# A language-model tower on one core: the filter network between the first groups, adjacency row blocks added on VectorE, seeds by square root

## The reference

```python
def _vgcn(word_emb, gv_ids, adj, W, b):
    ev = word_emb[gv_ids]
    H = jnp.einsum('bgh,bhd->bgd', adj, ev)
    g = H.mean(axis=1)
    return jax.nn.relu(g @ W.T + b)
# tok: x = concat(emb + pos, g1, g2, g3); y = layernorm(x @ W_proj.T + b_proj) * gamma + beta
def _implicit_filter(L, w1, b1, w2, b2, w3, b3, freq, deltas_abs):
    z, t = _pos_emb(L)
    h = jnp.sin(freq * (z @ w1.T + b1))
    h = jnp.sin(freq * (h @ w2.T + b2))
    h = h @ w3.T + b3
    decay = jnp.exp(-t[:, None] * deltas_abs[None, :])
    return h * (decay + SHIFT)
# attn: h = h + fft_conv(u, k) + u * bias, with u = layernorm(h)
# ffn:  top_k of xf @ Wr.T with k = 2, softmax over the two, gelu experts, weighted sum, h = h + out
```

## Time and profile before

| | |
|---|---|
| median of three runs | 1069.83 us (1067.11 to 1072.25) |
| profiled execution | 1066.09 us, of which the span of instructions is 1064.2 |
| group stage | the last projection ends at 376.8 us |
| conv, on TensorE | starts at 392.8 us |
| routing | about 443 to 514 us |
| first expert tile | 559 us |

### The profile page before, as it was taken

How to read it: one execution, slowest core, us unless ns; L and a number is a source line. 1 busy time by engine, 2 the same in 40 slices (tenths; PEclk the granted TensorE clock), 3 DMA queues, 4 the chain that set the end, 5 groups by cost and what they waited for, 6 DMA issues and landing times. The chain is left out here.

```text
span 1064.2 us, 22506 instructions
## 1 busy us (share of the span) xinstructions
PE 916.3 (86%) x7666; PEld 872.7 (82%) x7666; DVE 610.6 (57%) x1939; ACT 520.6 (49%) x1219; POOL 673.0 (63%) x592
## 2 busy tenths in 40 slices
PE   1999999999999939567259999999999999999993
PEld 0999999999999839567148899899889989999992
DVE  3046745666457664867864555556556655556561
ACT  2022222212223235698356666566656666666661
POOL 6767777677677000067015788778768768888864
PEclk9967655665557569879659999999999999999997
DMA  7427547266364339504944544764763463444442
GB/s 223 137 71 242 175 150 243 84 228 202 112 240 130 104 104 301 159 1 121 279 141 112 110 61 59 196 139 61 172 161 58 61 168 57 64 62 61 60 48 30
DMA packets 99495, 138.08 MB, mean 130 GB/s; under 512 B 13395, under 2 KB 81142, under 8 KB 97366
## 3 DMA queue, kind: packets, MB, share of 16 engines
q0 software_dynamic: 39552, 53.26, 26.1%
q1 hardware_dynamic: 58854, 73.40, 22.0%
q10 hardware_dynamic: 1008, 10.34, 2.7%
HBM read 98.14 MB, written 38.82 MB: 129 GB/s over the span
## 5 line engine op out<-in xcount | busy, mean ns | idle before, releaser
L893 ACT ACTIVATE Hs<-bank,U 128x256 bf16<-128x256 f32 x426 | 213.8, 502 | 176.6 <-PE bank L719 176.6
L518 POOL DMA_INDIRECT out<-Hs,id_s x142 | 235.7, 1660 | 64.9 <-issue 56.1
L1233 DVE TENSOR_TENSOR Hs<-Hs 128x512 bf16<-128x512 f32 x213 | 147.6, 693 | 174.9 <-ACT Hs L894 161.8
L484 POOL DMA_INDIRECT ev_g<-in_word_emb,ids_i x192 | 191.6, 998 | 71.4 <-issue 54.5
L894 ACT ACTIVATE Hs<-bank,U 128x256 f32<-128x256 f32 x426 | 216.2, 508 | 0.0
L509 POOL DMA_INDIRECT blob<-xtab_d,id_g x142 | 142.1, 1001 | 109.6 <-DVEq L1217 47.6
L734 PE MATMUL bank<-U,Hs 128*128 128x192 bf16 x852 | 210.0, 247 | 0.3 <-issue 0.3
L736 PE MATMUL bank<-U,Hs 128*128 128x192 bf16 x852 | 208.8, 245 | 0.0
L735 PE MATMUL bank<-U,Hs 128*128 128x192 bf16 x852 | 208.6, 245 | 0.0
L715 PE MATMUL bank<-blob,U 128*128 128x256 bf16 x426 | 117.1, 275 | 13.8 <-issue 11.8
L718 PE MATMUL bank<-blob,U 128*128 128x256 bf16 x426 | 117.1, 275 | 0.0
(11 more groups left out here) (192 smaller groups left out, 1699.9 us busy)
## 6 DMA issues: line engine op xcount, KB each, us to landing
adj_s<-in_adj SPq DMA_DIRECT2D x48, 256.0 KB, 7.6
ev_g<-kpad_d SPq DMA_DIRECT2D x24, 512.0 KB, 5.8
U<-blob_d SPq DMA_DIRECT2D x14, 771.0 KB, 4.9
wst<-in_wsrc SPq DMA_DIRECT2D x8, 1344.0 KB
blob_d<-blob ACTq DMA_DIRECT2D x7, 1443.0 KB, 5.6
U<-blob_d SPq DMA_DIRECT2D x14, 672.0 KB
xtab_d<-U SPq DMA_DIRECT2D x4, 1552.0 KB, 10.4
out<-Hs SPq DMA_DIRECT2D x4, 1536.0 KB, 10.9
```

The source lines that it names most:

```text
L484: pool.indirect_dma_start(ev_g[:, p, j, b, :], None, t["word_emb"], bass.IndirectOffsetOnAxis(ap=ids_i[:, 1 + j, i * Q + b:i * Q + b + 1], ...
L518: pool.indirect_dma_start(out, bass.IndirectOffsetOnAxis(ap=id_s[:, 2 * q + h:2 * q + h + 1], axis=0), yo[:, q % RX, h, :], None, compute_ ...
L893: f(hh[w][:, d, :], ps, ACT.Gelu, bias=bi[:, d:d + 1])
L1233: last = v.tensor_tensor(hl[w][:, c:c + 2, :], hf[w][:, c:c + 2, :], hh[w][:, c:c + 2, :], ALU.subtract)
```

## The change

The filter network's second and third layer move behind the first two groups: the second matmul behind the projection of group 0, the third before the projection of group 1, the sine and decay on ScalarE behind `graphs(0)`, VectorE's second argument and the taps behind `rows(0)`. Its sums move from bank 0 to bank 7 and its scratch from `ys` to the last eight batches of `Hs`. VectorE adds the four row blocks of each adjacency into the first (`row_sums`, two additions a group, the first of 128x768, the second of 128x384), and the column means read that block alone, one matmul a graph. ScalarE seeds the roots by a square root, VectorE takes its reciprocal. The share exponentials move from i = 6, 10, 14 to i = 9, 11, 14, and a dummy square root stands ahead of the first seeds.

```diff
@@ -538,28 +538,30 @@
             mm = nc.tensor.matmul
             pe.wait_ge(loaded, 16 * N_LOADS)
-            mm(bank[0][0:16, 0:128], w1T, net_z, start=True, stop=True).then_inc(filt_step, 1)
+            mm(bank[7][0:16, 0:128], w1T, net_z, start=True, stop=True).then_inc(filt_step, 1)
             nc.tensor.transpose(bank[1][:, 0:128], pos[:, 0:D0], cst[:, 0:128])
             nc.tensor.transpose(bank[1][0:D1, 128:256], pos[:, D0:D], cst[:, 0:128]).then_inc(pos_t, 1)
             pe.wait_ge(pos_ts, 1)
             mm(bank[2][:, 0:D], posT0[:, :], wp0[:, :], start=True, stop=False)
             mm(bank[2][:, 0:D], posT1[:, :], wp1[0:D1, :], start=False, stop=True).then_inc(pos_t, 1)
-            pe.wait_ge(filt_in, 1)
-            mm(bank[0][0:16, 128:256], w2T, sinb[:, 3, :], start=True, stop=True).then_inc(filt_step, 1)
-            pe.wait_ge(filt_in, 2)
-            mm(bank[0][:, 256:384], w3T[:, 0:D0], sinb[:, 4, :], start=True, stop=True)
-            mm(bank[0][0:D1, 384:512], w3T[:, D0:D], sinb[:, 4, :], start=True, stop=True).then_inc(filt_step, 1)
-            pe.wait_ge(kready, 2)
             pe.wait_ge(pos_done, 1)
             pe.wait_ge(cast_done, 1)
-            def column_means(n, i, p):
-                pe.wait_ge(adj_in[p], 16 * GRAPHS * n)
+            def filter_layer(n):
+                pe.wait_ge(filt_in, n)
+                if n == 1:
+                    mm(bank[7][0:16, 128:256], w2T, sinb[:, 3, :], start=True, stop=True).then_inc(filt_step, 1)
+                else:
+                    mm(bank[7][:, 256:384], w3T[:, 0:D0], sinb[:, 4, :], start=True, stop=True)
+                    mm(bank[7][0:D1, 384:512], w3T[:, D0:D], sinb[:, 4, :], start=True, stop=True).then_inc(filt_step, 1)
+                    pe.wait_ge(kready, 2)
+
+            def column_means(i, p):
+                pe.wait_ge(summed, i + 1)
                 after(pe, cs_ready, i)
                 for j in range(GRAPHS):
                     k = p * KG + j * Q
-                    for r in range(Q):
-                        last = mm(bank[0][:, k:k + Q], adj_s[:, p, j, r, :], mean_w[:, :], start=r == 0, stop=r == Q - 1)
+                    last = mm(bank[0][:, k:k + Q], adj_s[:, p, j, 0, :], mean_w[:, :], start=True, stop=True)
                 last.then_inc(colsum, 1)
             def turn_embeddings(it, i, p):
...
@@ -601,14 +603,19 @@
             def pair(it):
                 for p in range(2):
                     i = 2 * it + p
+                    opening = isinstance(it, int) and it == 0
                     turn_embeddings(it, i, p)
                     if not (isinstance(i, int) and i == NQ - 1):
-                        column_means(it + 1 + p, i + 1, 1 - p)
+                        column_means(i + 1, 1 - p)
                     graph_vectors(it, i, p)
                     graph_features(i)
+                    if opening and p == 1:
+                        filter_layer(2)
                     project(i, p)
-
-            column_means(1, 0, 0)
+                    if opening and p == 0:
+                        filter_layer(1)
+
+            column_means(0, 0)
             steps(pe, NQ // 2, pair, last=1)
...
@@ -752,15 +759,18 @@
             f(posT0[:, :], bank[1][:, 0:128], ACT.Copy)
             f(posT1[:, :], bank[1][0:D1, 128:256], ACT.Copy).then_inc(pos_ts, 1)
-            for n in range(2):
+            def filter_sine(n):
                 act.wait_ge(filt_arg, n + 1)
                 f(sinb[:, 3 + n, :], sinb[:, 2, :], ACT.Sin).then_inc(filt_in, 1)
+            def filter_decay():
+                trow = cst[:, 512:640]
+                f(dec[:, 0, :], trow, ACT.Exp, scale=filt[:, 0, 3:4])
+                f(dec[0:D1, 1, :], trow[0:D1, :], ACT.Exp, scale=filt[0:D1, 1, 3:4]).then_inc(dec_done, 1)
+
+            filter_sine(0)
             act.wait_ge(cast_done, 1)
             act.wait_ge(loaded, 16 * N_LOADS)
-            trow = cst[:, 512:640]
-            f(dec[:, 0, :], trow, ACT.Exp, scale=filt[:, 0, 3:4])
-            f(dec[0:D1, 1, :], trow[0:D1, :], ACT.Exp, scale=filt[0:D1, 1, 3:4]).then_inc(dec_done, 1)
             def column_copy(i, p):
                 act.wait_ge(colsum, i + 1)
...
@@ -802,6 +812,9 @@
                     if not (isinstance(i, int) and i == NQ - 1):
                         column_copy(i + 1, 1 - p)
                     graphs(i, p)
+                    if isinstance(i, int) and i == 0:
+                        filter_decay()
+                        filter_sine(1)
                     if p:
                         split_hi(it)
                     if not (isinstance(i, int) and i == 0):
...
@@ -832,9 +845,7 @@
                 first, n = PIECES[k]
                 b = slice(first, first + n)
                 act.wait_ge(var_ready, k + 1)
-                f(seed[:, 1, b], seed[:, 0, b], ACT.Ln, scale=-2.0).then_inc(log_done, 1)
-                act.wait_ge(log_done, k + 1)
-                f(seed[:, 2, b], seed[:, 1, b], ACT.Exp, scale=-0.5).then_inc(seed_ready, 1)
+                f(seed[:, 1, b], seed[:, 0, b], ACT.Sqrt, scale=-2.0).then_inc(seed_ready, 1)
             def row_parts(i):
                 p = i % 2
...
@@ -858,6 +869,7 @@
                 act.wait_ge(gap_ready, g + 1)
                 f(wsm[:, 1, bass.ds(g * GRP, GRP)], wsm[:, 0, bass.ds(g * GRP, GRP)], ACT.Exp).then_inc(exp_done, 1)
+            f(junk[:, :], mean_w[:, 0:1], ACT.Sqrt)
             seeds(0)
             seeds(1)
             row_parts(0)
...
@@ -868,8 +880,8 @@
                 turned_parts(i)
                 if i in (1, 4, 8):
                     seeds({1: 3, 4: 4, 8: 5}[i])
-                if i in (6, 10, 14):
-                    gap_exp((i - 6) // QG)
+                if i in (9, 11, 14):
+                    gap_exp((9, 11, 14).index(i))
             gap_exp(NG - 1)
             f(junk[:, :], mean_w[:, 0:1], ACT.Gelu)
...
@@ -930,10 +942,10 @@
             v.tensor_scalar(filt[0:D1, 1, 3:4], filt[0:D1, 1, 0:1], -1.0, None, ALU.mult).then_inc(cast_done, 1)
-            for n in range(2):
+            def filter_argument(n):
                 dve.wait_ge(filt_step, n + 1)
                 fence()
-                v.tensor_scalar(sinb[:, 0, :], bank[0][0:16, n * 128:(n + 1) * 128], net_cols[:, n:n + 1], net_cols[:, 2:3], ALU.add, ALU.mult)
+                v.tensor_scalar(sinb[:, 0, :], bank[7][0:16, n * 128:(n + 1) * 128], net_cols[:, n:n + 1], net_cols[:, 2:3], ALU.add, ALU.mult)
                 fence()
                 v.tensor_scalar(sinb[:, 1, :], sinb[:, 0, :], 1.0 / TWO_PI, MAGIC, ALU.mult, ALU.add)
                 fence()
...
@@ -947,16 +959,17 @@
                     src = sinb[:, 2, :]
                 fence()
                 v.tensor_scalar(sinb[:, 2, :], sinb[:, 2, :], 3.1415925, -3.1415925, ALU.min, ALU.max).then_inc(filt_arg, 1)
-            dve.wait_ge(filt_step, 3)
-            dve.wait_ge(dec_done, 1)
-
-            for c, n in ((0, D0), (1, D1)):
-                kk = kT[0:n, c, 0:S]
-                v.tensor_scalar(kk, bank[0][0:n, 256 + 128 * c:384 + 128 * c], filt[0:n, c, 1:2], 1.0 / NFFT, ALU.add, ALU.mult)
-                fence()
-                v.tensor_tensor(kk, kk, dec[0:n, c, :], ALU.mult)
-                fence()
-                v.tensor_tensor(kT[0:n, c, S - 1:S], kT[0:n, c, S - 1:S], filt[0:n, c, 2:3], ALU.add).then_inc(kready, 1)
+
+            def filter_taps():
+                dve.wait_ge(filt_step, 3)
+                dve.wait_ge(dec_done, 1)
+                for c, n in ((0, D0), (1, D1)):
+                    kk = kT[0:n, c, 0:S]
+                    v.tensor_scalar(kk, bank[7][0:n, 256 + 128 * c:384 + 128 * c], filt[0:n, c, 1:2], 1.0 / NFFT, ALU.add, ALU.mult)
+                    fence()
+                    v.tensor_tensor(kk, kk, dec[0:n, c, :], ALU.mult)
+                    fence()
+                    v.tensor_tensor(kT[0:n, c, S - 1:S], kT[0:n, c, S - 1:S], filt[0:n, c, 2:3], ALU.add).then_inc(kready, 1)
             dve.wait_ge(pos_t, 2)
             v.tensor_tensor(posb[:, :], bank[2][:, 0:D], bproj[:, :], ALU.add).then_inc(pos_done, 1)
...
@@ -1018,10 +1031,29 @@
                 v.tensor_tensor(lo_up, wst[:, 0:WI], hi_up, ALU.subtract)
                 v.tensor_tensor(lo_down, wst[:, WI:WE], hi_down, ALU.subtract).then_inc(w_lo, 1)
+            def row_sums(i, p, turn):
+
+                dve.wait_ge(adj_in[p], 16 * GRAPHS * turn)
+                a = adj_s[:, p, :, :, :]
+                v.tensor_tensor(a[:, :, 0:2, :], a[:, :, 0:2, :], a[:, :, 2:4, :], ALU.add)
+                fence()
+                v.tensor_tensor(a[:, :, 0, :], a[:, :, 0, :], a[:, :, 1, :], ALU.add).then_inc(summed, 1)
+
+            row_sums(0, 0, 1)
+            row_sums(1, 1, 1)
+            filter_argument(0)
+
             def pairs(it):
+                if not (isinstance(it, int) and it == NQ // 2 - 1):
+                    row_sums(2 * it + 2, 0, it + 2)
                 rows(2 * it, 0)
+                if isinstance(it, int) and it == 0:
```

(6 more changed lines are left out.)

12 lines of the change are left out of this document (6 added, 6 removed).

## The result

The changed kernel takes 1053.99 us (median of 4 runs, 1049.88 to 1054.8); the kernel before, measured with it, 1068.47 us (4 runs, 1064.65 to 1072.25). The ratio is 0.9857, 95% interval 0.9811 to 0.9902: faster by 14.5 us. 25.2 us and 1044.6 us were forecast; the median lies in the range of 1037 to 1060. The profiled execution of the changed kernel took 1053.4 us, its span is 1051.6 us; against the profiled execution of before (1066.1) that is 12.7 us less.

What follows compares the result with a forecast made beforehand. TensorE was taken as the bound, GpSimd only 1.3 us a group behind. Group stage 23.7 us plus routing 1.5 gave a 25.2 us gain, from the median of 1069.8 to 1044.6 us; range 1037 to 1060.

Steps and rivals of the forecast that it cites:

- The bound passes from TensorE to GpSimd: Group stage: TensorE's period falls to 15.6 to 19.2 us, under GpSimd's 20.0; most of 32 to 62 us freed is uncollectable.
- the same two parts: Group stage's 23.7 us gain: GpSimd's last issue from 346.7 to 338.5, and a shorter tail to the last projection.
- GpSimd's end: Last gather issue, 346.7 before: less 11.2 us of waiting for TensorE, plus 3 us of stretching by additions, 338.5.
- The tail behind the last issue: Group stage's end: 2.6 us landing, 3.4 us matmuls, 8.6 us to the last projection, at 353.1.
- rival 1: Group stage: additions block GpSimd's issues in full, 1.2 us a group; gain only 9, 1061 us; chance 0.09.
- rival 2: Group stage: late adjacency loads become the bound, 21.5 us a group; gain about 12, 1058 us; chance 0.08.
- The signs set down beforehand: Trace marks expected: no GpSimd wait for TensorE, last issue 336 to 342, conv near 369, three table loads, earlier row parts.
- three signs that were to show the forecast wrong: Additions meeting issues over 1.3 us each group; additions awaiting adjacency with TensorE behind; graph-vector copies still every 21 us.
- Cost 0: First groups, network moved: vectors 14 us earlier, some 8 us of TensorE stall in group 1, gathers not delayed, 4 us cover.
- rival 3: Group stage: opened gaps keep TensorE at half clock, period 22.4 us; slower, 1078 us; chance 0.03.
- Routing: Square-root seeds and fewer table loads save ScalarE 15 us, but the loop with VectorE leaves a 1.5 us gain, between 0 and 15.
- I followed the queues with the durations of before: Routing: old durations put choices(0) 2.4 us earlier, row parts of group 8 1.8 and group 12 1.4 earlier.

Runs made afterwards that it cites:

- experiment 6: Kernel before with only the filter network moved between the first groups, no additions, routing as before; 1059.89 us, one run.
- Experiment 3: Changed kernel loading only 64 of 2688 expert weights a partition from the second expert on; 1044.9 us, one run.
- experiment 2: Changed kernel with every adjacency addition made twice; 1060.68 us, one run.
- Experiment 4: Changed kernel with SyncE loading a pair's first adjacency before waiting for the expert store, the second after the expert's load; 1047.89 us, ratio 0.9777.
- experiment 1: Changed kernel with the routing of before: logarithm and exponential seeds, no reciprocal, share exponentials at their old places; 1049.88 us, ratio 0.98.
- Experiment 10: Changed kernel with GpSimd writing zeros for routing's low parts instead of subtracting; 1122.18 us on the chip where the kernel before takes 1182.8.
- experiment 7: Experiment 4's kernel without the Newton step that refines routing's scale, three VectorE instructions a piece fewer; 1041.56 us, ratio 0.9746.

## Why the prediction was right, and what it missed

**The bound passes from TensorE to GpSimd: right.** The waits for TensorE are gone, TensorE stands idle a fifth of the time, and of the 47 us that left its queue the stage gave 20. Of the 20.3, GpSimd's own end explains only 3.6 (346.7 to 343.2). The rest is backlog: before, TensorE was 30.1 us behind the last gather when the gathers were through, and now it is 13.4. The prediction's sum has the same two parts, 8.2 and 15.5 us.

**Mis-sized term: GpSimd's end.** "Less 11.2, plus 3" gave 338.5; it came to 343.2. The 11.2 us of waiting for TensorE did go (experiment 6 keeps 8.9 of them, the changed kernel has none). The additions stretched issues by 3.1 us, as taken; the weight subtraction by 5.1 less. What was missing is the waits for landings, 9.0 us more than before: 346.7 - 11.2 + 3.1 + 0.4 - 5.1 + 9.0 = 342.9, where 0.4 is what other instructions stretch. Once GpSimd no longer waits for TensorE, it meets the next thing in line, and the prediction had named no such thing for it. Experiment 3 shows the cause: without the expert's burst, the last issue ends at 335.4. The tail behind the last issue was 13.4 us for a forecast of 14.6, so 356.6 came out for 353.1. That GpSimd's end missed by no more than 4.7 us is in part luck, for nobody had forecast the 5.1 us that the weight subtraction gave back.

**The additions as a hold on GpSimd (rival 1).** As a mechanism it is real, as experiment 2 shows, and at the size taken it doesn't decide. The rows that the prediction held against it were no evidence: the issue at 210.27 starts 0.15 us before the end of L1019 and the one at 219.06 0.21 us before that of L1007, so there was next to nothing to wait for; by the rule read in experiment 2 they fit it. In a sentence apart: the Trainium skill (SBUF — State Buffer, "Who interferes with whom") infers that tensor_tensor leaves descriptor generation alone; the rows at 230.04 above and 235.47 of experiment 2 are against that, and the measurement decides.

**The adjacency loop (rival 2): a wait, no bound.** The 14.0 us of VectorE's waits are the delay that it described. Experiment 4 takes 11 us of them away and the end moves by 2.0, as much as GpSimd's own waits give, and hardly more than two profiles of one group stage differ.

**The signs set down beforehand: mixed.** GpSimd no longer waits for TensorE, and TensorE's gaps end on landings (15.7 us); VectorE's first rows of group 1 come at 72.46 (near 73); from the roots on there are three table loads. The first row parts come 2.3 us earlier after the conv's end (forecast 2), the last ones 2.2 later (forecast 1 to 2 earlier). The last issue (343.2 for 336 to 342) and the conv (372.7 for 369) came late. And two of the three signs that were to show the forecast wrong did appear: additions wait for adjacency with TensorE behind them (14.0 and 12.6 us), and the copies of the graph vectors still come every 20.9 us on average (34.05 to 347.97), before 21.3. Neither shows the forecast wrong. The first is a wait off the bound, as experiment 4 shows; for the second, "every 21 us" lay too near the 20.0 us of GpSimd's issues, to which 0.6 us of stretching and 0.7 us of landings a group are added.

**The start: right.** Graph vectors 0 at 34.05 (forecast 34), ScalarE at the second sine until 59.34 (about 60), TensorE idle 10.0 us up to 60.99 (57 to 62, some 8 us), 1.9 us for the taps, projection 1 behind. No gather waited for it. "Cost 0" is right for the changed kernel, and the move is worth more than nothing: alone 5.8 us (experiment 6), beside the additions 3.5, by one profile each.

**TensorE's clock (rival 3): no.** 0.66 of full clock over two groups, against 0.57 and 0.67 in the earlier trace rows.

**Routing: the step failed.** Forecast was a gain of 1.5 us, measured is a loss of 1.6, and experiment 1 puts 1.4 us of it on the routing part (0.4 to 1.9 over all profiles). ScalarE's load was cut as counted (12 table loads in the six seeds gone, one for exp left), and bought nothing, as the loop's pace is VectorE's. The failed step is "I followed the queues with the durations of before", and it fails from its first result on: choices(0) was to start 2.4 us earlier and starts 2.0 us later (27.2 us after the first variances, before 25.2), and the row parts of group 8 and 12, forecast 1.8 and 1.4 us earlier, come 0.9 and 0.6 later. Earlier seeds move VectorE's short steps under GpSimd's subtractions, where 0.16 us becomes 0.60 and 1.04. The third scales are done 13.7 us after the first variances, before 10.7. Experiment 10 takes the reading GpSimd work away and the steps are short again; experiment 7 takes some of the steps away and gets 4.8 us. In sentences apart: the Trainium skill (SBUF — State Buffer, same section) says that a VectorE instruction with two inputs in SBUF contends with a GpSimd instruction that reads SBUF, and not with one that only writes it. By that rule the trace agrees: stretched beside L500 and L501, 0.16 us beside the memset of experiment 10.

**The experts: open.** From the first tile to the end it is 505.0 us in the trace of before and 511.2 after, with the same instructions. On the chips of the usual speed the two kernels without additions have 504.2 and 505.0 us, the eight with them 508.0 to 512.7; on the slow chip the order is the other way round (517.7 without, 510.8 to 513.4 with). One profile each, whole executions of one kernel 5 to 8 us apart, and no mechanism in the rows that tells them apart: not settled. The forecast had counted nothing there. Without it the gain at the first expert tile is 18.9 us, and the forecast's 25.2 less 3.5 (group stage) and less 3.1 (routing) is 18.6.

## What to carry to other kernels

When an engine is relieved, the gain ends where the next one's own clock stands; count that engine's fixed steps between instructions, its backlog at the end, and then ask what it will wait for next, transfers first. A step that is moved changes which instructions run beside each other on VectorE and GpSimd, and short steps on a chain can grow several times over when they fall under a longer read of the other; durations of before hold only for the company of before. Relieving an engine that is not on the chain buys nothing until the chain itself is shortened, here by fewer short VectorE steps: 4.8 us in routing.

## What the runs showed of the hardware

- A VectorE addition of 0.95 us held an indirect gather's issue for 0.64 us (235.47 in experiment 2). In 81 of 89 cases an issue that started under a two-input addition or subtraction was stretched by what was left of it less 0.13 us; in the other eight it started within 0.04 us of VectorE's start and VectorE was stretched instead, by 0.04 to 0.07 us. Doubling the additions raised the stretching of all issues from 9.3 to 18.8 us.
- Short VectorE steps of 4 elements a partition, 0.16 us alone, took 0.60 and 1.04 us under GpSimd subtractions of 0.67 and 1.15 us, and ended within 0.03 us of these. A one-input VectorE instruction of 8 elements took 0.65 us under a GpSimd cast, too; it took 0.17 us in the kernel before, where no cast ran beside it.
- Gathers' landings were late beside the expert's burst: 10.7 us of waiting, 0.4 without the burst.
- One chip runs the group stage of the same kernel 101 us longer and its routing as fast as the others (116.1 us). GpSimd's issues take 0.95 us there too; what is long is TensorE's stands between graph vectors, 74 us in all (none in the first trace of before), and behind them GpSimd's waits for TensorE, 102.1 us where they were 13.3. The profile doesn't say what TensorE stands for. The change is worth more there: experiment 10, whose group stage is that of the changed kernel, ends it at 433.1 us, the kernel before at 477.8.
